# A scatter that adds in place of a gather, an add and a scatter, in the routed part of a mixture of experts

## The reference

```
shared = geglu(xf, w1s, w2s, w3s)                 # every row
idx = argmax(xf @ Wg, axis=-1)                    # one of 8 experts for each row
final = y_e of the row's own expert               # geglu(xf, W1[e], W2[e], W3[e])
x = x + shared + final
```

## Time and profile before

| | us |
|---|---|
| median of 3 runs | 3009.29 |
| lowest and highest of them | 3006.54, 3010.42 |
| profiled execution, its own time | 3007.97 |
| span of the profiled execution | 3006.2 |
| PE busy in the span | 2802.5 (93%) |
| DVE busy | 1614.2 (54%) |
| ACT busy | 810.7 (27%) |
| POOL busy | 116.0 (4%) |

### The profile page before, as it was taken

The page is one execution under the profiler, slowest core; times in us unless marked ns, Lnnn a source line. Parts: engine busy times, 40 slices in busy tenths (PEclk is TensorE's granted clock), DMA queues, the critical chain, the costliest instruction groups (busy, mean ns, idle before and its releaser), DMA issues. The chain is left out here.

```text
span 3006.2 us, 35349 instructions
## 1 busy us (share of the span) xinstructions
PE 2802.5 (93%) x13066; PEld 1848.9 (62%) x13066; DVE 1614.2 (54%) x2626; ACT 810.7 (27%) x949; POOL 116.0 (4%) x128
## 2 busy tenths in 40 slices
PE   6999289779999999999999999999999699979998
PEld 4555178646666666666666666666666465666666
DVE  6776768765555555555555555555555643213111
ACT  3211266332222322222223222232222221011111
POOL 0000000000000000000000000000000000000122
PEclk9999689879999999999999999999999799989999
DMA  4200300111011110111101101011010201023995
GB/s 142 61 27 29 80 1 1 61 42 63 34 46 56 38 63 34 40 62 36 65 34 40 62 34 68 34 40 62 34 40 1 76 1 22 8 97 141 322 345 193
DMA packets 111428, 197.82 MB, mean 66 GB/s; under 512 B 25581, under 2 KB 72815, under 8 KB 111356
## 3 DMA queue, kind: packets, MB, share of 16 engines
q1 hardware_dynamic: 102472, 176.38, 18.1%
q0 software_dynamic: 7344, 15.37, 1.5%
q10 hardware_dynamic: 1540, 5.12, 0.4%
HBM read 166.38 MB, written 27.40 MB: 64 GB/s over the span
## 5 line engine op out<-in xcount | busy, mean ns | idle before, releaser
L1025 PE MATMUL rails_ps_acc<-rails_w_hi,rails_hid_hi 128*125 128x512 f16 x2560 | 971.6, 380 | 8.1 <-DVE rails_hid_lo L947 8.1
L1025 PE MATMUL rails_ps_acc<-rails_w_lo,rails_hid_hi 128*125 128x512 f16 x2560 | 971.4, 379 | 0.0
L1025 PE MATMUL rails_ps_acc<-rails_w_hi,rails_hid_lo 128*125 128x512 f16 x2560 | 971.3, 379 | 0.0
L982 DVE SCALAR_TENSOR_TENSOR keep_X<-rails_ps_acc,rails_out_scale,keep_X 125x512 f32<-125x512 f32 x640 | 479.7, 750 | 708.0 <-PE rails_ps_acc L1025 708.0
L870 ACT ACTIVATE rails_act_f<-rails_ps_h,keep_scale_gelu 128x1000 f32<-128x1000 f32 x160 | 175.0, 1094 | 1198.0 <-PE rails_ps_h L1011 1198.0
L1025 PEld LDWEIGHTS rails_ps_acc<-rails_w_hi,rails_hid_lo 128*125 128x125 f16 x2560 | 349.9, 137 | 203.6 <-issue 1.0
L1025 PEld LDWEIGHTS rails_ps_acc<-rails_w_hi,rails_hid_hi 128*125 128x125 f16 x2560 | 349.9, 137 | 200.8 <-issue 9.3
L1025 PEld LDWEIGHTS rails_ps_acc<-rails_w_lo,rails_hid_hi 128*125 128x125 f16 x2560 | 349.9, 137 | 191.1 <-issue 0.8
L947 DVE SCALAR_TENSOR_TENSOR rails_hid_lo<-rails_act_f,keep_scale_hidden,rails_hid_hi 128x1000 f16<-128x1000 f32 x160 | 200.6, 1254 | 52.4 <-ACT rails_hid_hi L878 52.4
L878 ACT ACTIVATE rails_hid_hi<-rails_act_f,keep_scale_hidden 128x1000 f16<-128x1000 f32 x160 | 180.6, 1129 | 31.2 <-ACT rails_act_f L870 29.8
L762 PE MATMUL att_ps_o<-att_zh,counts_room 125*125 125x257 f32 x800 | 175.5, 382 | 6.2 <-DVE counts_room L687 6.2
(11 more groups left out here) (272 smaller groups left out, 2483.5 us busy)
## 6 DMA issues: line engine op xcount, KB each, us to landing
rails_w_land<-cproj SPq DMA_DIRECT2D x32, 2048.0 KB
ffn_w<-W SPq DMA_DIRECT2D x51, 1024.0 KB
rails_xs<-rails_xt_hi SPq DMA_DIRECT2D x64, 78.1 KB
rails_xs<-rails_xt_lo SPq DMA_DIRECT2D x64, 78.1 KB
keep_X<-x SPq DMA_DIRECT2D x10, 448.0 KB
z_d<-open_z SPq DMA_DIRECT2D x10, 448.0 KB
att_zh<-z_d SPq DMA_DIRECT2D x4, 1120.0 KB
xn_d<-ffn_xn SPq DMA_DIRECT2D x10, 448.0 KB
```

What stands on the lines that cost most here:

```text
L982: nc.vector.scalar_tensor_tensor(to, ps_acc[0:P, j, :], out_scale[b][0:P, 0:1], to, ALU.mult, ALU.add).then_inc(acc_used, 1)
L1025: mm = nc.tensor.matmul(ps_acc[0:P, j, :], hid[k2][l][:, k, (j // 2) * P:(j // 2 + 1) * P], w[b][r][:, k, cols], start=(k == 0 and n == 0) ...
```

## The change

`gather_res` and the scratch array `xs_d` are gone. The ten own tiles are stored straight to `out`, so that `out` holds x + shared. `slot_out` copies the two PSUM banks to `res` with no add, and the scatter adds `res` to the rows of `out` (`compute_op=ALU.add`). What kept a `res` buffer from being overwritten too early, the wait of `gather_res` on POOL, becomes a wait on DVE ahead of `slot_out`: it waits until the scatter of slot s - 2 has landed. The two clearings of `res` on POOL at the stage's start are gone. POOL's order over the slots is now gather(s + 3), scatter(s).

```diff
-                    nc.gpsimd.memset(res[b][:], 0.0).then_inc(blank, 1)
-                pool.wait_ge(blank, 4)
+                pool.wait_ge(blank, 2)
...
-                def gather_res(s):
-                    if s >= 2:
-                        pool.wait_ge(out_stored[s % 2], 16 * ((s - 2) // 2 + 1))
-                    nc.gpsimd.indirect_dma_start(out=res[s % 2][:], out_offset=None, in_=xs_d,
-                                                 in_offset=bass.IndirectOffsetOnAxis(ap=tokens[:, s:s + 1], axis=0),
-                                                 bounds_check=NODES - 1, oob_is_err=False).then_inc(res_in[s % 2], 16)
-
                 def scatter(s):
                     pool.wait_ge(y_taken, 2 * (TILES + s) + 2)
                     nc.gpsimd.indirect_dma_start(out=out, out_offset=bass.IndirectOffsetOnAxis(ap=tokens[:, s:s + 1], axis=0),
                                                  in_=res[s % 2][:], in_offset=None, bounds_check=NODES - 1,
-                                                 oob_is_err=False).then_inc(out_stored[s % 2], 16)
+                                                 oob_is_err=False, compute_op=ALU.add).then_inc(out_stored[s % 2], 16)
...
                 for t in range(TILES):
                     pool.wait_ge(xs_stored[t], 32)
-                gather_res(0)
-                gather_res(1)
                 gather(2)
                 for s in range(SLOTS):
                     if s + 3 < SLOTS:
                         gather(s + 3)
                     scatter(s)
-                    if s + 2 < SLOTS:
-                        gather_res(s + 2)
...
-                    rows_to(act, xs_d[t * P:(t + 1) * P, :], X[:, t, :], xs_stored[t])
+                    rows_to(act, out[t * P:(t + 1) * P, :], X[:, t, :], xs_stored[t])
...
                 def slot_out(s):
                     u = TILES + s
-                    dve.wait_ge(res_in[s % 2], 16 * (s // 2 + 1))
+                    if s >= 2:
+                        dve.wait_ge(out_stored[s % 2], 16 * ((s - 2) // 2 + 1))
                     for h in range(2):
                         cols = slice(h * BANK, (h + 1) * BANK)
                         dve.wait_ge(y_sum, 2 * u + h + 1)
-                        nc.vector.tensor_tensor(res[s % 2][:, cols], ps_y[:, h, :], res[s % 2][:, cols], ALU.add)\
-                          .then_inc(y_taken, 1)
+                        nc.vector.tensor_copy(res[s % 2][:, cols], ps_y[:, h, :]).then_inc(y_taken, 1)
```

More of the change, by code:

```diff
@@ L1301, in _, with experts @@
                         mm.then_inc(summed, 1)
-def experts(nc, X, mean_var, rstd, ident, w1s, w2s, w3s, Wg, W1, W2, W3, xn_d, xs_d, out):
+def experts(nc, X, mean_var, rstd, ident, w1s, w2s, w3s, Wg, W1, W2, W3, xn_d, out):
     TE = [P, TILES, EXPERTS]
@@ L1359, in experts @@
         blank, xg_in = c.sem("blank"), [c.sem(f"xg_in{k}") for k in range(2)]
-        res_in, out_stored = [c.sem(f"res_in{k}") for k in range(2)], [c.sem(f"out_stored{k}") for k in range(2)]
+        out_stored = [c.sem(f"out_stored{k}") for k in range(2)]
         made, upper_set, step, hot_set, ranked = [c.sem(n) for n in ("made", "upper_set", "step", "hot_set", "ranked")]
@@ L1721, in program @@
     z_d = scratch("z_d", (NODES, DIM))
-    xn_d, xs_d = scratch("xn_d", (NODES, DIM)), scratch("xs_d", (NODES, DIM))
+    xn_d = scratch("xn_d", (NODES, DIM))
     with ExitStack() as ctx:
@@ L1750, in program @@
         layer_stats(nc, "stats3", stat_parts, mean_var, rstd)
-        experts(nc, X, mean_var, rstd, ident, w1s, w2s, w3s, Wg, W1, W2, W3, xn_d, xs_d, out)
+        experts(nc, X, mean_var, rstd, ident, w1s, w2s, w3s, Wg, W1, W2, W3, xn_d, out)
 def kernel(x, src, dst, L0_gnn_W, L0_gnn_a_l, L0_gnn_a_r, L0_ffn_rail_maker, L0_ffn_rail_up_proj, L0_ffn_w_cproj,
```

## The result

The kernel after takes 2994.84 us (median of 5, 2994.47 to 2996.96); the kernel before took 3009.29 (3005.86 to 3010.42). The ratio is 0.9954, 95% interval 0.9941 to 0.9967. 2995.5 had been forecast.

What follows compares the result with a forecast made beforehand. It took late gathers, held on POOL behind gather_res waiting for scatters, to stall PE in the slots. 13.2 + 0.5 + 0.1 = 13.8 us off the profiled 3007.97 gives 2994.2, a median of 2995.5 us; range 2992 to 3013.

Steps and rivals of the forecast that it cites:

- The removed wait: Slots 0 to 14: with gather_res gone from POOL, gathers land before turn needs them; 13.2 us go.
- T(14) - T(0): Time between the starts of slot_out's second half in slots 0 and 14; forecast to fall from 173.25 to near 160 us.
- the 6.7 us to spare: Between the slots: time from a gather's landing at T + 11.6 to its turn at T + 18.3.
- The start of the slots: Start of the slots: gather(2), no longer behind two gather_res, comes 2.6 us earlier; 0.5 us go.
- The landing of an adding scatter: Scatter in the slots: latency taken as about 10 us, between bounds of 8.0 and 22.7.
- Rival C: Slots: rows of an add do not overlap inside an engine, so slower, +35 us, 3044 us; chance 0.15.
- The engines' time of the add: DMA engines in the slots: +13 us if the add doubles the scatter's time, offsetting -13 us from the removed gather_res.
- slot_out: Last slot's slot_out on DVE: a copy of 0.6 us replaces the add of 0.69; -0.1 us.
- The end: After the last slot_out: path as before, one scatter with no rows; no change.
- The spare of the loads: Weight loads in the slots: issued 25.2 us before use, taking 5.4 us, so 20 us to spare.
- Rival B: Slots: the DMA engines' work is the real limit, so no change, 3009 us; chance 0.10.

Runs made afterwards that it cites:

- the order: Kernel before with only POOL's order changed: gather(s + 4) right behind scatter(s), ahead of gather_res(s + 2); 2995.92 us, ratio 0.9959.
- the third buffer: Kernel before with a third res buffer, so gather_res need not wait for the scatter just issued; 2997.26 us, ratio 0.9961.
- the wait put back: Kernel after, with POOL waiting for scatter(s) to land before issuing gather(s + 4); 3004.19 us, ratio 0.9978.
- one gather added: Kernel after with one more gather a slot, behind the scatter, whose rows nobody reads; 3010.11 us, ratio 1.0006.
- the transfer from SBUF to SBUF: Kernel after with one more plain transfer a slot, 128 rows of 2880 bytes, SBUF to SBUF; 3005.92 us, ratio 0.9987.
- the one from HBM: Kernel after with one more plain transfer a slot, 128 rows of 2880 bytes, read from HBM; 3008.11 us, ratio 0.9997.
- Without the add: Kernel after with compute_op left out, a plain scatter in place of the adding one; 2993.93 us, ratio 0.9948.

## Why the prediction was right

The removed wait. Confirmed by three edits that have nothing else in common (the add, the order, the third buffer), all at T(14) - T(0) = 160.11 us, where 160.0 was worked out from one unstalled slot; and by the wait put back, which loses 9.8 us. The gather follows the scatter by 1.9 us and not by 1.3, since the adding scatter takes longer to issue; of the 6.7 us to spare some 6 were left.

The start of the slots. -0.5 forecast, -0.6 measured.

The landing of an adding scatter. About 10 us was taken between bounds of 8.0 and 22.7. It is a little less: 8.8 us in the median where the trace has it, some 9.5 by the wait put back. Rival C needs 17.2, and doesn't occur. The rule of the Trainium skill, page "DMA: Bandwidth & Descriptors", section "Two DMAs through the same engine are not ordered", that the descriptors of one queue are pipelined, agrees with it: rows done one after the other would have given 22.7 us by the estimate of the prediction.

The engines' time of the add. +13 us if it doubles the scatter's: 12.6 measured in its own queue, and the scatter about doubled. No row had told that it would be twice and not three times.

slot_out. -0.1 was wrong: DVE's copy of 512 columns from PSUM takes 0.69 us as its add does. The nearest row had been one of ACT, and it did not carry over.

The end. "As before" missed 0.8 us. From the last slot_out to the end of the span it is 8.2 and 8.3 us in the profiles of the order and of the third buffer, as before, and 7.4 to 7.5 in those of the kernel after, so it goes with what the change removes and the other two keep; how is open.

The spare of the loads, 20 us, is the step that failed, though the sum does not contain it. It was taken as a stock that a busier ring could draw on: 175 us of work before, 20 to spare, so that an add could cost 3 us more a scatter before it hurt. Both numbers of that spare were wrong. The 25.2 us from issue to use are those of slot 3, whose w1 waits only for the up of slot 0. From slot 4 on, w1 stands on SP's queue behind the w3 of the slot before, which waits for a down, and in the kernel after 19.9 to 21.8 us are left. And a load of w1 and w2 does not take 5.4 us in the full ring. In the kernel after, SP issues the w2 of slot 12 at 2906.73 us, it lands 18.6 us later, at 2925.4, and PE uses it at 2927.12, 1.8 us later (timeline of PE):

```profile
2927.12 0.60 PE L1634 MATMUL ffn_ps_a<-ffn_w,ffn_xt 128*128 128x256 f32 x2
```

The other four whose landing the trace has (slots 3, 6, 9 and 15) were there 13.4, 7.1, 5.9 and 5.7 us ahead of their use. So the spare was nearly used up already. Adding one transfer of 1.0 us a slot took 12.0 of the 13.1 us that were won in the slots. The 391 GB/s of the earlier trace rows were no measure of what fits either: the order alone moves 57.3 MB in 163 us, 352 GB/s, with both queues' shares at 101.4%, and the w2 of its slot 12 lands 1.6 us ahead of its use. The line, from 2797 to 2960 us of that run:

```profile
DMA packets 38216, 57.32 MB, mean 352 GB/s; under 512 B 3099, under 2 KB 31294, under 8 KB 38207
```

Rival B was therefore nearer than its 0.10. The bound of the DMA engines is not where it was put, at 175 + 20 us of work, but hardly above the 161 us of the kernel after. The kernel after and the order alone just pass under it. Had the add held the engines for 1 us more a slot, the time would have been some 12 us longer, about 3007 (an estimate from the run with one gather added). That the forecast still came out was luck in this one point: the add happened to take no more than the gather_res that went. The Trainium skill's figure of about 358 GB/s from HBM (page "DMA: Bandwidth & Descriptors", section "Specifications") happens to lie close to the 352, but the transfer from SBUF to SBUF, 168.3 us as the one from HBM, shows that in this stretch another thing is full.

A misreading without effect: POOL waits for a landing not 13 but 15 times before. Two waits of gather_res, 16.1 us together, are put down to turn in the trace, which had long been done; the one that ends at 2857.66 is one of them.

## What to carry to other kernels

A wait in an in-order queue costs by what stands behind it, not by its length: look for the transfer behind the wait that does not need it, and move it ahead before anything is rewritten; here a few moved lines gave what the whole change gave. When a gain lets an engine run without pause, ask of the transfers not whether they are waited for but whether their engines have time left; the first sign is the issue of a load that takes several microseconds on its queue. An accumulating scatter is free only while the engines have that time, since it took about twice a plain one here.

## What was not expected of the hardware

An indirect scatter with an add lands 0.5 to 1.3 us later than a plain one (8.8 and some 9.5 us against 8.3 in a busy ring), of which its longer issue on POOL (1.59 us against 1.01) is a good part, but it takes the DMA engines some 1.9 us against 0.9 for its rows. Two transfers of one size cost the same in a full ring whether they read HBM or SBUF (168.3 us both). The full ring can be seen before PE stands still: in the kernel after the w2 of a slot takes SP 0.5 us to issue in slot 4, and 7.7 us in slot 12, with PE at full pace. Without the add it never takes more than 2.6 us from slot 3 on:

```profile
2814.34 0.53 SPq L1386 DMA_DIRECT2D ffn_w<-W  x1
...
2906.73 7.73 SPq L1386 DMA_DIRECT2D ffn_w<-W  x1
```
